# Value products of an attention quad: two key chunks per visit to the 32-column tiling instead of one

## The chip, the cores and the metric

The kernel runs on one core of one Trainium2 chip. The metric is the device time of one execution in microseconds (us). A measured time is the median of several executions; beside it stands one execution that was taken with the hardware profiler, and every row of a trace comes from that one.

## The reference

The input is 8 sequences of 512 tokens with 128 features. There is one attention block with 16 heads of 8 features, and one mixture-of-experts block. Cut to what matters here:

```python
qkv = (x @ w_qkv + b_qkv).reshape(B, 16, S, 24)      # B=8, S=512
q, k, v = jnp.split(qkv, 3, axis=-1)
attn = softmax(einsum('bhqd,bhkd->bhqk', q, k) / sqrt(8))
vals = einsum('bhqk,bhkd->bhqd', attn, v)
x = layernorm(x + vals @ w_out + b_out)
# then: a shared expert for each token, 8 routed experts of which each token
# takes 2, a weighted sum, and a second layernorm
```

## The kernel before

**Quads and stages.** The attention works through 32 quads: 8 batches (b) of 4 quads (i = 0 to 3), and a quad is four heads over 512 query and 512 key positions. All engines run the same loop of stages (`run_stages`, line 308). Stages 8 to 27 are a hardware loop of five batches, the others are written out. Stage q = 4b + i does work for several quads at once, as a software pipeline: the score maxima of quad q+2, the exponentials of quad q, the value products of quad q-1, and small jobs for others. In this document "quad 0" to "quad 3" mean the stages with i = 0 to 3.

**A stage on TensorE** (`attention_tensor`, line 955) has eight steps, `at` = 0 to 7. Two steps belong to one value of j (= `at // 2`), and u = `at % 2`. Each step issues four matrix products of 512 columns in bfloat16:
- A, A' (`score_a`, line 971): scores for the row maximum, into a pair of PSUM banks of `scoreA`. There are two pairs, one for even and one for odd steps. VectorE takes the maximum over a pair with one instruction (line 915) and so frees it. So A of step n waits until the maximum of step n-2 is done.
- B, B' (`score_b`, line 985): scores the other way round, each into one of the two banks of `scoreB`. ScalarE turns each into exponentials in SBUF (line 882, 512 elements per partition) and frees the bank. So B of step n waits for the exponential of B of step n-1, and B' for that of B'.

**Small jobs** follow the four products of a step (`Jobs.at`, line 71). They share one PSUM bank, `shared`, so a job on TensorE waits until the reader of the job before it is done (line 499). In every quad: mT at step 1 (line 520; VectorE reads it after its maximum of step 1, lines 595 and 597), valsT at step 3 (line 524; VectorE reads it after its maximum of step 3), xT at step 4 (line 502), and the three projections qkv at step 6 (lines 508, 509, 513; read by ScalarE). In quad 1 also counts at step 2 (line 493; VectorE reads it with lines 380 and 383) and oT at step 7; in quad 2 proj at step 0; in quad 3 x1T at step 5 and gate at step 7. VectorE also has the routing's arithmetic: `choose` in quad 0 (line 318) and `place` in quads 1 and 2 (line 393), small instructions put behind its maxima at odd steps. Batches 2 and later have routing; batches 1 and later have the layer norm's statistics.

**The value products** are at the end of a step (lines 999 to 1008). At u = 1, so behind steps 1, 3, 5 and 7, four products for key chunk j are issued, one for each head h. Their weights have 32 columns each and go to columns 32h to 32h+31, so that the four stand beside each other in the array, and their results to 32 partitions of the bank `pvp` each. The operands are float32, and the trace has two MATMUL records for each product (8 for a chunk). Every other product of a step uses all columns. The four chunks of a quad add up in PSUM (start at j = 0, stop at j = 3). ScalarE copies the finished bank to `pv_sb` at the start of the next stage (line 874). The first products of a quad wait for `exp_done` (the exponentials of the quad are finished), `v_ready` (the values, from GpSimd) and `pv_copied` (the bank has been copied).

Below, a "visit" is the run of column-tiled value products between two other products.

```python
                    score_a(at, 0)
                    score_b(at, 0)
                    score_a(at, 1)
                    score_b(at, 1)
                    for kind in jobs.at(b, i, at):
                        pe_job(pe, kind, b, i)
```

After the attention (about 512 us into the span) come the shared expert and 72 blocks of routed rows. The change does not touch them.

Of the kernel before, what the change touches and what calls it, by code (L numbers as in the profile page):

```python
# [103 lines left out]
def layer(nc, x, w_qkv, b_qkv, w_out, b_out, wg, ws1, ws3, ws2, we1, we3, we2, out):  # L104
# [26 lines left out]
    with ctx:  # L131
        def sb(name, shape, dt=F32):
            return ctx.enter_context(nc.sbuf_tensor(name, shape, dt))

        def psum(name, shape):
            return ctx.enter_context(nc.psum_tensor(name, shape, F32))
# [42 lines left out]
        v = sb("v", [P, 2, 4, NCH, 32])  # L179
        prob = sb("prob", [P, 2, 4, NCH, 512])  # L180
# [52 lines left out]
        pvp = psum("pvp", [P, 512])  # L233
# [52 lines left out]
        def need(eng, s, value):  # L286

            if isinstance(value, int) and value <= 0:
                return
            eng.wait_ge(s, value)  # L290
            if not isinstance(value, int) and eng.engine in ALONE:


                eng.sem_inc(passed, 1)

        def has(b, i, ahead):

            return not isinstance(b, int) or 0 <= 4 * b + i + ahead < QUADS
# [9 lines left out]
        def run_stages(eng, stage):  # L308

            for s in range(-4, 8):  # L310
                stage(s // 4, s % 4)
            with eng.Fori(2, B - 1) as b:
                for i in range(4):
                    stage(b, i)
            for s in range(QUADS - 4, QUADS + 1):
                stage(s // 4, s % 4)
# [355 lines left out]
        def turn_x(pe, b):  # L672

            pe.wait_ge(x1_loaded[b], 16)

            need(pe, xT_low_done, b)
            for c in range(NCH):
                ins = pe.transpose(xT_bank[:, c * P:(c + 1) * P], xsum[:, b, c, :], ident[:])
            ins.then_inc(xT_ready, 1)
# [275 lines left out]
        def attention_tensor(pe):  # L955

            pe.wait_ge(setup, 2)

            def stage(b, i):
                q = 4 * b + i  # L960
                if has(b, i, 2):

                    pe.wait_ge(stack_loaded[i % 2], 16 * STACK_DMAS * (2 * b + i // 2 + 2))
                def score_a(at, c):

                    if has(b, i, 2):
                        st, j, qc = (i + 2) % 4, at // 2, at % 2 * 2 + c

                        if c == 0:
                            need(pe, max_done, 8 * (q + 2) + at - 1)  # L970
                        ins = pe.matmul(scoreA[:, at % 2, c], qs[0:KR, st, j, qc * P:(qc + 1) * P],  # L971
                                        ks[0:KR, st, j, :], start=True, stop=True)
                        if c == 1:
                            ins.then_inc(a_ready, 1)

                def score_b(at, c):

                    if has(b, i, 0):
                        j, kc = at // 2, at % 2 * 2 + c
                        if at == 0 and c == 0:  # L980

                            pe.wait_ge(m_loaded, 32 * (q + 1))

                        need(pe, exp_done, 16 * q + 2 * at + c - 1)
                        pe.matmul(scoreB[:, c], ks[0:KM, i, j, kc * P:(kc + 1) * P], qs[0:KM, i, j, :],  # L985
                                  start=True, stop=True).then_inc(b_ready, 1)

                for at in range(8):
                    j, u = at // 2, at % 2
# [6 lines that stand above are left out]

                    if isinstance(b, int) and q == QUADS and at == 4:
                        turn_x(pe, 0)
                    if u == 1 and has(b, i, -1):
                        if j == 0:  # L1000
                            pe.wait_ge(exp_done, 16 * q)
                            pe.wait_ge(v_ready, q)
                            need(pe, pv_copied, q - 1)
                        for h in range(4):
                            ins = pe.matmul(pvp[32 * h:32 * h + 32, :], v[:, (i - 1) % 2, h, j, :],  # L1005
                                            prob[:, (i - 1) % 2, h, j, :], start=(j == 0), stop=(j == 3))
                        if j == 3:
                            ins.then_inc(pv_done, 1)

            run_stages(pe, stage)  # L1010


# [535 lines left out]
```

## Time and profile before

| what | value |
|---|---|
| median of 3 executions | 717.0 us (715.78 to 718.37) |
| profiled execution | 719.39 us, of which the span from first to last instruction is 717.2 us |
| mean granted TensorE clock | 0.979 of full speed; full in the steady attention |
| attention's value products | from 58.8 us to about 511.9 us in the span |
| a batch of four quads in the steady loop | 58.2 us |

The profiled execution took 2.4 us more than the median. A time for the changed kernel is to be read against the median, while durations and starts come from the profiled execution. In the timeline a row is: start, duration, engine, line, operation, output<-inputs, count; in square brackets how long the engine was idle before it, and what ended this. Rows for MATMUL run into each other: a product of 512 columns lasts 0.38 us in the records while the next one starts 0.22 us behind it. The distance from start to start is what TensorE's time is counted in. PEld is the load of weights.

### The profile page before, as it was taken

The page shows a single profiled execution, that of the slowest core. Times are in us where ns is not written, and L with a number is a line of the kernel's source. Part 1 is how long each engine was busy: PE and PEld are TensorE (multiplying, and loading weights), DVE is VectorE, ACT ScalarE, POOL GpSimd, SP SyncE. Part 2 cuts the span into 40 slices and gives each one's busy share as a digit, 9 for nine tenths or more (in the row PEclk, how much of TensorE's full clock was granted, in tenths as well). Part 3 has the DMA queues.
Part 4 walks back from the last instruction along what each step waited for, and adds up shares of the span by engine and source line. Part 5 has one row for each costly group of instructions (what it writes and reads, how often), then busy time and mean ns, then how long its engine had stood idle before and what let it go on. Part 6 is the DMA issues. An engine that isn't in the chain of part 4 may idle for free.

```text
span 717.2 us, 16568 instructions
## 1 busy us (share of the span) xinstructions
PE 649.3 (91%) x4593; PEld 312.3 (44%) x4594; DVE 543.9 (76%) x1208; ACT 427.0 (60%) x973; POOL 273.5 (38%) x418
## 2 busy tenths in 40 slices
PE   1899999999999999999999999998999898788870
PEld 1242333333343434334343334232488676666650
DVE  4965777779988997997997998876587566666651
ACT  1055767766777676766777677667342455555541
POOL 3112312322144243434225414505155265665562
PEclk9999999999999999999999999999899999998995
DMA  4357577354333334234323333301320233433321
GB/s 79 69 127 170 112 148 149 79 103 95 83 74 87 59 86 97 57 56 110 85 48 82 85 84 74 75 2 56 108 60 29 63 83 106 142 114 112 111 73 59
DMA packets 161848, 62.58 MB, mean 87 GB/s; under 512 B 110586, under 2 KB 155516, under 8 KB 161808
## 3 DMA queue, kind: packets, MB, share of 16 engines
q1 hardware_dynamic: 154112, 48.55, 30.5%
q0 software_dynamic: 5648, 13.26, 6.2%
q10 hardware_dynamic: 2048, 0.27, 0.3%
q8 instruction: 21, 0.34, 0.2%
q14 instruction: 19, 0.16, 0.1%
HBM read 38.04 MB, written 24.26 MB: 87 GB/s over the span
## 4 chain that ended last, share of the span: by engine, by line
PE 64%; DMA 9%; issue 8%; DVE 7%; POOL 5%; ACT 4%; SPq 1%; POOLq 0%; ACTq 0%; DVEq 0%
PE pvp L1005 17%; PE scoreB L985 16%; PE scoreA L971 15%; DMA y_dram<-prob 3%; DVE mx L915 2%; POOL y_dram L1162 2%; ACT prob L882 2%; DMA parts_dram<-parts 2%; PE shared L524 2%; DMA prob<-slots_dram 2%; PE shared L513 2%; PE scoreB L1490 1%; DMA ks<-parts_dram 1%; PE shared L508 1%; PE shared L532 1%
## 5 line engine op out<-in xcount | busy, mean ns | idle before, releaser
L915 DVE TENSOR_REDUCE mx<-scoreA 128x2 f32<-128x1024 f32 x256 | 305.8, 1220 | 69.8 <-PE scoreA L971 67.3
L882 ACT ACTIVATE prob<-scoreB 128x512 f32<-128x512 f32 x512 | 279.5, 600 | 119.0 <-PE scoreB L985 114.5
L971 PE MATMUL scoreA<-ks,qs 72*128 72x512 bf16 x512 | 206.0, 410 | 13.3 <-DMA ks<-parts_dram 10.9
L985 PE MATMUL scoreB<-qs,ks 74*128 74x512 bf16 x512 | 201.2, 396 | 6.3 <-ACT prob L882 3.0
L1005 PE MATMUL pvp<-prob,v 128*32 128x512 f32 x1024 | 139.8, 619 | 0.8 <-ACT pv_sb L874 0.8
L971 PEld LDWEIGHTS scoreA<-ks,qs 72*128 72x128 bf16 x512 | 51.0, 102 | 155.1 <-DVE mx L915 72.1
L809 POOL CAST parts<-qk 128x256 bf16<-128x256 f32 x32 | 12.7, 395 | 217.7 <-ACT v_raw L562 198.8
L1162 POOL DMA_INDIRECT y_dram<-prob x72 | 71.5, 993 | 60.6 <-ACT prob L1374 31.5
L985 PEld LDWEIGHTS scoreB<-qs,ks 74*128 74x128 bf16 x512 | 49.8, 99 | 102.0 <-ACT prob L882 80.3
L487 POOL DMA_INDIRECT slots_dram<-rows,slot_i x64 | 63.3, 989 | 26.7 <-issue 17.4
L1321 DVE TENSOR_TENSOR prob<-scoreA,prob 128x256 f32<-128x256 f32 x72 | 30.4, 422 | 31.6 <-ACT prob L1368 31.3
L1490 PE MATMUL scoreB<-w,prob 128*128 x288 | 45.4, 282 | 0.1
L1374 ACT ACTIVATE prob<-scoreB,prob 128x128 f32<-128x128 f32 x72 | 26.3, 366 | 31.1 <-PE scoreB L1490 29.8
L1368 ACT ACTIVATE prob<-scoreA 128x256 f32<-128x256 f32 x72 | 27.4, 381 | 22.8 <-PE scoreA L1469 22.8
L1477 PE MATMUL pvp<-ident,prob 128*128 128x128 f32 x144 | 29.1, 284 | 12.2 <-DVE prob L1326 11.6
L1490 PEld LDWEIGHTS scoreB<-w,prob 128*128 128x128 f32 x288 | 38.8, 196 | 0.4 <-issue 0.2
L1467 PE MATMUL scoreA<-w_high,ebT_high 128*128 x72 | 35.3, 491 | 0.9 <-DVE ebT_low L1274 0.9
L1005 PEld LDWEIGHTS pvp<-prob,v 128*32 128x32 f32 x1024 | 20.5, 109 | 30.1 <-issue 28.5
L558 ACT ACTIVATE qk<-shared,bq 128x128 f32<-128x128 f32 x64 | 20.0, 364 | 17.8 <-PE shared L513 12.0
L1326 DVE COPY prob<-pvp 128x256 f32<-128x256 f32 x72 | 29.9, 415 | 0.6 <-PE pvp L1477 0.3
L1477 PEld LDWEIGHTS pvp<-ident,prob 128*128 128x128 f32 x144 | 16.3, 143 | 31.1 <-DVE prob L1321 18.1
L635 POOL TENSOR_SCALAR veps<-mv 128x4 f32<-128x4 f32 x8 | 1.8, 222 | 72.3 <-DVE mv L617 72.3
(172 smaller groups left out, 882.6 us busy)
## 6 DMA issues: line engine op xcount, KB each, us to landing
qs<-parts_dram SPq DMA_DIRECT2D x96, 96.0 KB
parts_dram<-parts SPq DMA_DIRECT2D x32, 192.0 KB, 3.7
slots_dram<-blank POOLq DMA_DIRECT2D x9, 520.0 KB
prob<-slots_dram SPq DMA_DIRECT2D x72, 65.0 KB, 1.9
ks<-parts_dram SPq DMA_DIRECT2D x64, 64.0 KB
prob<-y_dram SPq DMA_DIRECT2D x8, 512.0 KB, 3.2
ks<-parts_dram SPq DMA_DIRECT2D x32, 96.0 KB
xin<-in_L_attn_x SPq DMA_DIRECT2D x32, 64.0 KB, 2.1
```

The source lines that it names most:

```text
L487: pool.indirect_dma_start(slots_dram, bass.IndirectOffsetOnAxis(ap=slot_i[:, j, t:t + 1], axis=0), rows[:, t, j, :], None).then_inc(scatte ...
L882: act.activation(prob[:, i % 2, j, 2 * u + c, :], scoreB[:, c], ACT.Exp, scale=SCALE).then_inc(exp_done, 1)
L915: dve.tensor_reduce(mx[:, i % 2, at // 2, at % 2 * 2:at % 2 * 2 + 2], scoreA[:, at % 2], AX.X, ALU.max).then_inc(max_done, 1)
L971: ins = pe.matmul(scoreA[:, at % 2, c], qs[0:KR, st, j, qc * P:(qc + 1) * P], ks[0:KR, st, j, :], start=True, stop=True)
L985: pe.matmul(scoreB[:, c], ks[0:KM, i, j, kc * P:(kc + 1) * P], qs[0:KM, i, j, :], start=True, stop=True).then_inc(b_ready, 1)
L1005: ins = pe.matmul(pvp[32 * h:32 * h + 32, :], v[:, (i - 1) % 2, h, j, :], prob[:, (i - 1) % 2, h, j, :], start=(j == 0), stop=(j == 3))
L1162: pool.indirect_dma_start(y2_dram, bass.IndirectOffsetOnAxis(ap=eb[:, r, D:D + 1].bitcast(I32), axis=0), yo[:, r, :], None, bounds_check=T ...
L1321: dve.tensor_tensor(gated[:, r % 2, :], scoreA[:, 0, r % 2, F:2 * F], silu[:, r % 2, :], ALU.mult) \
L1326: dve.tensor_copy(gatedT[:, (r - 1) % 2, :], pvp[:, 0:F]).then_inc(gT_copied, 1)
L1467: pe.matmul(h, ebT_high[:, r % 2, 0:P], high, start=True, stop=False)
L1477: ins = pe.transpose(pvp[:, c * P:(c + 1) * P], gated[:, (r - 1) % 2, c * P:(c + 1) * P], ident[:])
L1490: ins = pe.matmul(y, gatedT[:, r % 2, c * P:(c + 1) * P], w2_flat[:, bass.ds(e * NFC * D + c * D, D)], start=(c == 0), stop=(c == NFC - 1))
```

## The change

The visits behind steps 1 and 5 are taken away. The visit behind step 3 issues the products of chunks 0 and 1, that behind step 7 those of chunks 2 and 3. The three waits of a quad's first value product stand ahead of the visit behind step 3. Number, shape and order of the value products stay the same.

```diff
-                    if u == 1 and has(b, i, -1):
-                        if j == 0:
+                    if u == 1 and j % 2 and has(b, i, -1):
+                        if j == 1:
                             pe.wait_ge(exp_done, 16 * q)
                             pe.wait_ge(v_ready, q)
                             need(pe, pv_copied, q - 1)
-                        for h in range(4):
-                            ins = pe.matmul(pvp[32 * h:32 * h + 32, :], v[:, (i - 1) % 2, h, j, :],
-                                            prob[:, (i - 1) % 2, h, j, :], start=(j == 0), stop=(j == 3))
+                        for kc in (j - 1, j):
+                            for h in range(4):
+                                ins = pe.matmul(pvp[32 * h:32 * h + 32, :], v[:, (i - 1) % 2, h, kc, :],
+                                                prob[:, (i - 1) % 2, h, kc, :], start=(kc == 0), stop=(kc == 3))
                         if j == 3:
                             ins.then_inc(pv_done, 1)
```

## Rows read from the trace of the kernel before

**Rows 1.** The page: busy time of each engine; shares of the last chain by line.
```profile
PE 649.3 (91%) x4593; PEld 312.3 (44%) x4594; DVE 543.9 (76%) x1208; ACT 427.0 (60%) x973; POOL 273.5 (38%) x418
...
PE pvp L1005 17%; PE scoreB L985 16%; PE scoreA L971 15%; DMA y_dram<-prob 3%; DVE mx L915 2%; POOL y_dram L1162 2%; ACT prob L882 2%; DMA parts_dram<-parts 2%; PE shared L524 2%; DMA prob<-slots_dram 2%; PE shared L513 2%; PE scoreB L1490 
```

**Rows 2.** Busy time by stretch: quads 2, 3, 0 and 1 of the steady loop.
```profile
245.17:259.55 14.38, 14.35 (x119) 5.78 (x115) 13.48 (x30) 9.90 (x21) 3.20 (x7) 1.00 0.28 60
259.55:274.77 15.22, 15.07 (x123) 6.11 (x119) 12.28 (x23) 10.60 (x24) 7.45 (x11) 1.00 0.39 91
274.77:288.49 13.72, 13.58 (x111) 4.71 (x107) 12.26 (x24) 9.89 (x21) 5.56 (x8) 1.00 0.45 101
288.49:303.38 14.89, 14.75 (x119) 5.58 (x115) 13.64 (x32) 10.40 (x23) 5.95 (x11) 1.00 0.29 58
```

**Rows 3.** The page's costliest groups: maxima, exponentials, value products.
```profile
L915 DVE TENSOR_REDUCE mx<-scoreA 128x2 f32<-128x1024 f32 x256 | 305.8, 1220 | 69.8 <-PE scoreA L971 67.3
L882 ACT ACTIVATE prob<-scoreB 128x512 f32<-128x512 f32 x512 | 279.5, 600 | 119.0 <-PE scoreB L985 114.5
...
L1005 PE MATMUL pvp<-prob,v 128*32 128x512 f32 x1024 | 139.8, 619 | 0.8 <-ACT pv_sb L874 0.8
```

**Rows 4.** Timeline, end of the attention: chunks 2 and 3 of the last quad.
```profile
509.95 1.93 PE L1005 MATMUL pvp<-prob,v 128*32 128x512 f32 x16
...
510.41 0.13 PEld L1005 LDWEIGHTS pvp<-prob,v 128*32 128x32 f32 x4 [0.30 <-issue]
...
511.81 0.50 PE L1437 MATMUL scoreA<-ebT_high,w_high 128*128 128x512 f32 x1
```

**Rows 5.** Timeline of quad 0, first half: steps 0 and 1 and the visit.
```profile
274.77 0.39 PE L971 MATMUL scoreA<-ks,qs 72*128 72x512 bf16 x1
...
275.49 2.16 ACT L882 ACTIVATE prob<-scoreB 128x512 f32<-128x512 f32 x4
275.63 2.38 DVE L915 TENSOR_REDUCE mx<-scoreA 128x2 f32<-128x1024 f32 x2 [1.83 <-PE scoreA L971]
...
276.14 0.39 PE L985 MATMUL scoreB<-qs,ks 74*128 74x512 bf16 x1
...
276.63 0.39 PE L985 MATMUL scoreB<-qs,ks 74*128 74x512 bf16 x1
...
277.06 1.06 PE L1005 MATMUL pvp<-prob,v 128*32 128x512 f32 x8
...
278.06 0.39 PE L971 MATMUL scoreA<-ks,qs 72*128 72x512 bf16 x1
```

**Rows 6.** Timeline of quad 0, second half: its start, step 5, its visit.
```profile
281.60 0.39 PE L971 MATMUL scoreA<-ks,qs 72*128 72x512 bf16 x1
...
282.91 2.35 DVE L915 TENSOR_REDUCE mx<-scoreA 128x2 f32<-128x1024 f32 x2
...
283.38 0.39 PE L985 MATMUL scoreB<-qs,ks 74*128 74x512 bf16 x1
...
283.70 1.07 PE L1005 MATMUL pvp<-prob,v 128*32 128x512 f32 x8
...
284.70 0.39 PE L971 MATMUL scoreA<-ks,qs 72*128 72x512 bf16 x1
```

**Rows 7.** Timeline of quad 1: counts, its read, valsT, start of the second half.
```profile
292.83 0.40 PE L493 MATMUL shared<-both,lower 128*128 128x32 f32 x2
...
293.98 0.19 DVE L383 COPY count<-shared 128x32 f32<-128x32 f32 x1
...
294.23 0.66 PE L524 MATMUL shared<-ident,pv_sb 128*128 128x128 f32 x4
...
295.81 0.39 PE L971 MATMUL scoreA<-ks,qs 72*128 72x512 bf16 x1
```

**Rows 8.** Timeline of the last quad with exponentials: two steps, no A.
```profile
492.88 0.60 PE L985 MATMUL scoreB<-qs,ks 74*128 74x512 bf16 x2
493.31 2.17 ACT L882 ACTIVATE prob<-scoreB 128x512 f32<-128x512 f32 x4 [0.72 <-PE scoreB L985]
```

## The prediction

> **What bounds the kernel now.** I read the page first. TensorE is busy for 91% of the span, VectorE for 76%, ScalarE for 60%, and the chain that ended last names the value products at 17% and the two kinds of scores at 16% and 15% [rows 1]. Next the busy time by stretch, one for each quad of the steady loop: TensorE is busy in nearly all of it (13.58 of 13.72 us in quad 0), but VectorE in 12.26 to 13.64 us of 13.72 to 15.22 [rows 2]. So TensorE sets the pace with VectorE just behind it. Then the groups: a maximum takes 1.22 us, an exponential 0.60 [rows 3]. Last the timeline, where I count from start to start.
>
> **What a visit costs.** The last B' ahead of the visit in quad 0 starts at 283.38, the visit at 283.70, the next A at 284.70 [rows 6]. Between two score products stand 0.22 us, so going in costs 0.32 - 0.22 = 0.10, and a visit 1.00. How two chunks in a row do shows at the end of the attention, where no scores stand between them: 16 records from 509.95, the next product at 511.81, which is 1.86 us against 2 x 1.00 [rows 4]. A chunk adds 0.86 and coming out costs 0.14. A merge saves one way in and one out, 0.10 + 0.14, say 0.23 us. There are 1024 records, 8 for each of 128 visits [rows 3]; 64 merges, of which one is in effect already there, leave 63 x 0.23 = **14.5 us** of TensorE's time to be had at most. Waits of the first visit (exponentials, values, copied bank) come later than now and can only shrink. No DMA, job or instruction of another engine is moved, and SP and POOL keep their order.
>
> A rule speaks against this price. The Trainium skill's "TensorE: Matmul & The Clock Gate" (Part 3, the mechanism) says that a weight load overlaps products in flight only when it goes to other rows of the array, and these loads use all rows. The rows say otherwise: the four loads at 510.41 lie inside the running products, and the 1.86 us has room for none outside. By the rule the sum would be worse by some 16 us (a rival below).
>
> **What the visits cover.** Now to what a visit does for the others. Taking B of one step and B of the next, the loop through one bank is: product to exponential 0.43 (492.88 to 493.31 [rows 8]), exponential 0.60 [rows 3], and 0.06 until the next product starts. That is 1.08 us for a step, and four products in a row need only 4 x 0.22 = 0.88. For VectorE a step costs 1.19 (two maxima in 2.38 [rows 5]). So TensorE outruns both inside a run of steps, and the visit is when they catch up. After a one-chunk visit the first step runs free and the second waits (B at 276.14, 1.37 behind the half's first A, where 1.10 would be free [rows 5]). Take visit 1 away, and steps 2 and 3 run at the others' pace too.
>
> **First half of a quad** (steps 0 to 3, first A = 0). B and B' of step 1 start at 1.37 and 1.86 as now [rows 5]. Those of step 2 follow 1.08 later (2.45, 2.94), those of step 3 at 3.53 and 4.02; mT, 0.11 long, lies in a wait. A of step 2 needs maximum 0, done at 275.63 + 1.19, so 2.05: it is not late. A of step 3 needs maximum 1 at 3.24: starts at 3.30, which moves B' to at most 4.06. The scores end at 4.28, valsT takes 0.53, the visit 1.86: **6.67** against 281.60 - 274.77 = 6.83 now [rows 5, 6], so -0.16. A quad without routing has 6.63 against 6.75: -0.12.
>
> **Second half** (A of step 4 = 0). xT fits in as now. Exponential 5 ends at 2.36 and 2.88, so step 6 has B at 2.42, B' at 2.94; qkv takes 0.93, step 7 0.88, into the visit at 5.06, **6.92** at the end, against 6.89 now: +0.03. The waits of step 6, which visit 2 used to cover, take back all of the 0.23.
>
> **Quad 0 with routing.** VectorE has `choose` between the maxima and starts maximum 4 at 282.91 whatever TensorE does (it is without a gap from maximum 2 on), done at 284.09. A of step 6 could now start at 283.44 but waits to 284.15; now visit 2 fills that time, to 284.70 [rows 6]. From 284.15 on: step 6 0.88, qkv 0.93, step 7 0.88, way in 0.10, visit 1.86 gives 288.81, against 288.49 now: **+0.32**.
>
> **Quad 1 with routing** is the costliest. counts waits until VectorE has read mT (it starts at 292.83), and valsT until VectorE has read counts (293.98 + 0.19, it starts at 294.23) [rows 7]. Both waits are 0.2 us or less today, with visit 0 ahead of them. That chain does not get shorter by moving visit 0 behind it. It comes 0.18 earlier (VectorE's step 7 and 0 come up earlier), so valsT starts at 294.05, 0.58 to the visit, 1.86: A of step 4 at 296.49 against 295.81, +0.68 [rows 7]. In the second half oT waits for ScalarE's read of qkv and ends 7.61 later against 7.57. So it leaves at +0.72, of which quad 1 adds **+0.40**.
>
> **Quads 2 and 3.** In quad 2 proj (0.89 us) stands in step 0 and lets the others catch up; the same walk gives -0.24 and +0.03: **-0.21**. In quad 3 VectorE's first maximum comes at 1.18, holding A of step 2 to 2.42 and A of step 3 to 3.59: +0.05; x1T's read holds qkv by 0.17 in the second half, and the half gives -0.06: **-0.01**.
>
> **The sum.** A batch: 0.32 + 0.40 - 0.21 - 0.01 = +0.50. Five batches (2 to 6): +2.5. The first two quads of batch 7: +0.7. Its other two have no A and go at ScalarE's pace: eight exponentials in 2.17 a four, idle 0.72 before each four [rows 8], so 5.76 a half where now two visits cover them, 5.9 with one, less 0.2 at proj: +0.3. Quads 2 to 7 of the count, mostly without routing: -0.6. The first, at a clock half as fast with 1.86 for a one-chunk visit, so that nobody outruns anybody: -0.3. The last, without scores: -0.2. Together +2.4 us: **14.5 us of switching saved, about 17 us of waits exposed**. The profiled execution was 719.39, 2.4 above the median of 717.0; a difference carries over, so 717.0 + 2.4 = **719.4 us**.
>
> The unknown is how the waits add up: each of some four a quad was rounded with a latency of 0.06, and could be 0.02 to 0.10 (the exponential's measured answer is the nearest row); that and the phases it moves make 0.15 a quad, 4.5 us in all: 715 to 724 for this case.
>
> **Rivals.** *Gain (0.15).* The engines catch up in the two-chunk visit enough that waits stay as they are; speaking for it, VectorE has 0.9 to 2.9 us of a quad free and ScalarE 3.8 to 4.6 [rows 2]. Then 717.0 - 14.5 = 702.5; with half of it given back, 710. It is decided by step 6: does B start 1.1 or 1.3 behind the B of step 5. Against it: the loop of 1.08 is a latency, which no free time shortens. The Trainium skill's "TensorEngine Tiling (Array Packing)" (PSUM Bottleneck) speaks against it too: tiling makes TensorE faster but not the engines that empty PSUM, which may then be the limit. By it alone nothing of the 14.5 would arrive, and the time would stay at 717.0.
>
> *Loss by VectorE (0.17).* VectorE starves in the long visit (it has at most two maxima, 2.4 us, stored, often one) and falls behind in all quads as in quad 1. Then each of 30 quads adds 0.4: +12, 729 us. It decides where maximum 3 or 7 ends over 0.7 us before the next A pair is ready. For it: VectorE needs 13.5 of 14.38 us in quad 2. Against: in quad 2 the gap after maximum 7 exists already.
>
> *Weight loads exposed (0.03).* Loads of 0.13 [rows 4] ahead of the two later waves of each merged visit, 62 x 2 x 0.13 = 16 us on top: 735. By the rule of the Trainium skill's "TensorE: Matmul & The Clock Gate" named above it would be so.
>
> *The change saves no switch (0.03):* if what costs 0.14 is paid per chunk, a merged visit is 2.00 long: +9 on top, 728. Against it stands the 1.86 of [rows 4].
>
> **Numbers.** My case has 0.62. The range takes it and part of the gain case and of the loss case: 711 to 726. A measurement can tell 0.3%, 2.15 us. Faster: 0.15 from the gain and 0.04 of mine, 0.19. Slower: 0.17 + 0.06 and 0.25 of mine, 0.48. Same 0.33.
>
> **What would show it.** Merged visits of 16 records, 1.86 to the next product; 64 of them. Steps 2, 3 and 6 with B waiting for the exponential 0.1 to 0.3; in quad 0, A of step 6 waiting for the maximum by 0.7; in quad 1, counts waiting by 0.7 for the read of mT. Quads of 13.5 (no routing), 14.0, 15.3, 14.2 and 15.2 us (quads 0 to 3). A batch under 58.0 us would make me wrong, as would B of step 2 running free, or a merged visit near 2.0 us.

## The result, and the profile after

The changed kernel takes 729.08 us (median of 4 executions, 724.70 to 732.53) against 716.39 for the kernel before on the same chip (4 executions, 713.64 to 718.37): a ratio of 1.0157, 95% interval 1.0103 to 1.0211. (The ratios in this text are estimated from the single executions and are not the quotients of the medians; here the quotient is 1.0177, or 12.7 us.) It is slower, by more than the forecast of 719.4 and outside the range that ended at 726. Its profiled execution took 724.70 us, with a span of 722.5 and a mean granted TensorE clock of 0.975; the other three had 0.960, 0.964 and 0.969.

First the page of the changed kernel: busy time, shares of the last chain by line, the costliest groups.

```profile
PE 647.1 (90%) x4593; PEld 319.3 (44%) x4594; DVE 542.5 (75%) x1208; ACT 426.2 (59%) x973; POOL 274.9 (38%) x418
...
PE pvp L1006 14%; PE scoreB L985 13%; PE scoreA L971 13%; DVE mx L915 5%; DMA y_dram<-prob 3%; ACT prob L882 2%; PE shared L524 2%; PE scoreB L1491 2%; PE shared L513 2%; POOL y_dram L1163 1%; DMA prob<-slots_dram 1%; PE shared L508 1%; PE 
...
L915 DVE TENSOR_REDUCE mx<-scoreA 128x2 f32<-128x1024 f32 x256 | 303.9, 1217 | 76.7 <-PE scoreA L971 74.6
L882 ACT ACTIVATE prob<-scoreB 128x512 f32<-128x512 f32 x512 | 279.8, 602 | 98.2 <-PE scoreB L985 97.7
...
L1006 PE MATMUL pvp<-prob,v 128*32 128x512 f32 x1024 | 129.0, 623 | 0.0
```

Against [rows 1, 3]: the value products are as many (1024) and cover 10.8 us less, 129.0 for 139.8, since fewer switches lie among them. The chain now goes through the maxima for 5% of the span instead of 2%: TensorE waits for VectorE where it did not.

Next the busy time by stretch, for quads 2, 3, 0 and 1 of the same batch as in [rows 2]; the columns are the stretch, its length, the busy time of TensorE, weight loads, VectorE, ScalarE and GpSimd, the granted clock, the DMA share and GB/s.

```profile
248.13:262.30 14.17, 14.17 (x118) 5.90 (x115) 12.84 (x28) 9.90 (x21) 3.35 (x6) 1.00 0.30 61
262.30:277.45 15.15, 14.87 (x123) 6.26 (x119) 12.02 (x21) 10.48 (x23) 7.41 (x11) 1.00 0.41 92
277.45:291.49 14.04, 13.35 (x111) 4.94 (x107) 12.77 (x26) 9.90 (x21) 5.60 (x8) 1.00 0.43 99
291.49:307.13 15.64, 14.68 (x119) 5.79 (x115) 14.18 (x33) 10.39 (x22) 5.79 (x12) 1.00 0.27 55
```

| quad | before [rows 2] | forecast | after |
|---|---|---|---|
| 2 | 14.38 | 14.17 | 14.17 |
| 3 | 15.22 | 15.21 | 15.15 |
| 0 | 13.72 | 14.04 | 14.04 |
| 1 | 14.89 | 15.29 | 15.64 |
| batch | 58.21 | 58.71 | 59.00 |

Three quads came out as walked; quad 1 added 0.75 instead of 0.40. But 0.8 us more in each of some six batches is 5 us, not 12.7. The timeline shows the waits of quads 0 and 1, and something that the sum did not hold.

```profile
286.84 0.39 PE L971 MATMUL scoreA<-ks,qs 72*128 72x512 bf16 x1 [0.59 <-DVE mx L915]
...
289.63 1.92 PE L1006 MATMUL pvp<-prob,v 128*32 128x512 f32 x16
291.49 0.39 PE L971 MATMUL scoreA<-ks,qs 72*128 72x512 bf16 x1
...
294.00 0.39 PE L971 MATMUL scoreA<-ks,qs 72*128 72x512 bf16 x1 [0.17 <-DVE mx L915]
...
294.66 0.38 PE L985 MATMUL scoreB<-qs,ks 74*128 74x512 bf16 x1
295.72 0.40 PE L493 MATMUL shared<-both,lower 128*128 128x32 f32 x2 [0.68 <-DVE m L597]
...
299.53 0.39 PE L971 MATMUL scoreA<-ks,qs 72*128 72x512 bf16 x1
...
174.56 0.63 PE L493 MATMUL shared<-both,lower 128*128 128x32 f32 x2 [0.68 <-DVE m L597]
...
178.11 3.51 PE L1006 MATMUL pvp<-prob,v 128*32 128x512 f32 x16
...
354.72 0.40 PE L493 MATMUL shared<-both,lower 128*128 128x32 f32 x2 [0.68 <-DVE m L597]
...
357.62 2.51 PE L1006 MATMUL pvp<-prob,v 128*32 128x512 f32 x16
```

The merged visit is 291.49 - 289.63 = 1.86 us, as in [rows 4]. `A` of step 6 in quad 0 is idle for 0.59 before it starts, `counts` in quad 1 for 0.68. Counted from start to start these waits are longer: `counts` starts 1.06 behind `B'` at 294.66 where 0.22 would be free, so it loses 0.84, and `A` of step 6 loses 0.75 in the same way (286.84 against `B'` at 285.87). Then look at the same quad in two other batches, at 174 and 355: after the same wait, `counts` at 174.56 takes 0.63 us for 0.40, and the merged visit 3.51 and 2.51 instead of 1.92. The busy time by stretch around the second of them has the reason in its granted clock:

```profile
352.00:354.00 2.00, 1.84 (x8) 0.56 (x6) 2.00 (x3) 1.72 (x4) 1.72 (x6) 1.00 0.41 43
354.00:356.00 2.00, 1.32 (x8) 0.83 (x8) 1.93 (x6) 0.72 (x2) 1.23 (x1) 0.86 0.52 55
356.00:358.00 2.00, 2.00 (x10) 1.09 (x12) 1.51 (x3) 1.19 (x2) 0.00 (x0) 0.50 0.34 105
358.00:360.00 2.00, 2.00 (x16) 0.32 (x8) 1.11 (x7) 0.00 (x0) 0.00 (x0) 0.79 0.60 158
```

TensorE, busy 1.32 us of the 2 with the wait, falls from full clock (2.4 GHz) to the half (1.2 GHz) and works there for about 3 us; at 174 it is about 7 us. I call this a clock fall. The half quad with it took 9.57 us at 350 and 11.22 at 170, against 8.04 without: 1.5 and 3.2 us. From here on the text counts only falls between 70 and 490 us: in the last two quads or behind them every profile has stretches at half clock, the kernel before too (0.50 from 504 to 508 us). The attention's products end 6.8 us later than before (518.63 against 511.81); the two falls are 4.7 of that and the waits 2.1, where 2.4 was forecast. The part behind the attention is 1.5 us shorter (203.9 against 205.4), so the span has +5.3. The profiled execution before had 719.39, so the forecast stood for 721.8 there, and 724.7 came: +4.7 of falls, -0.3 of waits, -1.5 behind the attention. The other three executions have no profile, but a lower granted clock. A clock lower by 0.010 means 2% of the span, 14.5 us, at half clock, and half of that lost, about 7 us (an estimate); their mean lies 5.5 us above the profiled one. Where they lost the clock is not shown.

### The profile page after: what moved, and what is told of

Read it like the earlier page. It is cut to its first block, busy times and chain, and to the rows that moved or that the text cites. A ratio compares the mean times of both kernels' runs of the same rounds, so it can differ in the third digit from the quotient of the medians.

```text
span 722.5 us, 16563 instructions
## 1 busy us (share of the span) xinstructions
PE 647.1 (90%) x4593; PEld 319.3 (44%) x4594; DVE 542.5 (75%) x1208; ACT 426.2 (59%) x973; POOL 274.9 (38%) x418
## 4 chain that ended last, share of the span: by engine, by line
PE 59%; DVE 12%; issue 10%; DMA 7%; POOL 5%; ACT 4%; SPq 1%; POOLq 0%; DVEq 0%; ACTq 0%
PE pvp L1006 14%; PE scoreB L985 13%; PE scoreA L971 13%; DVE mx L915 5%; DMA y_dram<-prob 3%; ACT prob L882 2%; PE shared L524 2%; PE scoreB L1491 2%; PE shared L513 2%; POOL y_dram L1163 1%; DMA prob<-slots_dram 1%; PE shared L508 1%; PE pvp L1478 1%; PE scoreA L1468 1%; DMA parts_dram<-parts 1%
## 5 line engine op out<-in xcount | busy, mean ns | idle before, releaser
L1006 PE MATMUL pvp<-prob,v 128*32 128x512 f32 x1024 | 129.0, 623 | 0.0
L809 POOL CAST parts<-qk 128x256 bf16<-128x256 f32 x32 | 12.7, 396 | 217.7 <-ACT v_raw L562 198.5
L487 POOL DMA_INDIRECT slots_dram<-rows,slot_i x64 | 63.5, 992 | 27.5 <-issue 18.2
L1006 PEld LDWEIGHTS pvp<-prob,v 128*32 128x32 f32 x1024 | 27.4, 112 | 56.0 <-issue 50.8
L874 ACT ACTIVATE pv_sb<-pvp 128x512 f32<-128x512 f32 x31 | 18.5, 597 | 39.6 <-PE pvp L1006 39.6
```

Source lines behind the costliest of these rows:

```text
L487: pool.indirect_dma_start(slots_dram, bass.IndirectOffsetOnAxis(ap=slot_i[:, j, t:t + 1], axis=0), rows[:, t, j, :], None).then_inc(scatte ...
```

## The experiments

Theory 1, the one held after reading the result: the waits are those of the forecast, and the rest is clock falls behind the wait of `counts` in quad 1. Rival 2: the ratio is switching and waits alone, and the falls are chance that the kernel before has too. Rival 3: VectorE falls behind everywhere. Most kernels put the two `if` lines of the visit behind a table from step to key chunks; what differs is its content:

```diff
-                    if u == 1 and j % 2 and has(b, i, -1):
-                        if j == 1:
+                    chunks = visits(i).get(at, ())
+                    if chunks and has(b, i, -1):
+                        if chunks[0] == 0:
...
-                        for kc in (j - 1, j):
+                        for kc in chunks:
...
-                        if j == 3:
+                        if chunks[-1] == 3:
```

The kernel before is {1: 0, 3: 1, 5: 2, 7: 3} in this form ("four"), the changed one {3: 0 1, 7: 2 3} ("two"). The experiments ran on two other chips, the first four of the table on one, the others on the second. There the kernel before itself takes 741.35, 743.29 and 741.17 us (medians beside the three groups), so only ratios compare with the result; the times in us that the expectations of the first four runs give are meant for the first chip.

| run | visits | median us | ratio to before, 95% |
|---|---|---|---|
| again | two | 745.61 | 1.0040 (1.0007 to 1.0074) |
| first_pair | {3: 0 1, 5: 2, 7: 3} | 754.00 | 1.0157 (1.0105 to 1.0210) |
| second_pair | {1: 0, 3: 1, 7: 2 3} | 740.48 | 0.9968 (0.9928 to 1.0007) |
| not_quad1 | four in quad 1, else two | 737.07 | 0.9866 (0.9795 to 0.9937) |
| twin | four (one run) | 741.00 | - |
| cover | see below | 759.73 | 1.0263 (1.0185 to 1.0341) |
| filler | two, with products in the wait | 738.60 | 0.9933 (0.9897 to 0.9970) |
| pool_light | two, lighter split (one run) | 737.56 | - |
| best_b | four in quad 1, three in quad 0, else two | 731.82 | 0.9871 (0.9781 to 0.9960) |
| only_quad1 | two in quad 1, else four | 758.35 | 1.0226 (1.0110 to 1.0341) |
| early | {1: 0 1, 5: 2 3} | 768.36 | 1.0313 (1.0204 to 1.0423) |
| again_b | two | 745.57 | 1.0057 (1.0015 to 1.0098) |

### The change once more: again, again_b

> The changed kernel once more, in more rounds, to see how its executions spread. Theory 1 (waits in fixed places, of which the wait of counts in quad 1 also lets TensorE's clock fall in some batches): about 728 us, single executions from 724 to 733, and the mean granted clock between 0.96 and 0.975, lower in the longer executions, against 0.979 before. Theory 2 (the long visit starves ScalarE and VectorE everywhere alike, the clock has no part): the executions lie within 2 us of each other, with one clock.

> The changed kernel beside the others on this chip. Ratio 1.004 if ScalarE is late in quad 3 on this chip too (B of step 5 then waits over 1 us in the kernel before and 0.45 here), 1.016 if it is not. The clock falls after the wait of counts in one to six batches of a profile.

The change is slower here too, but by 0.4 and 0.6%, less than the 1.6% of the first chip. The falls are there: in the profile of again three batches took 62.54, 60.90 and 60.91 us, the others 58.70 to 59.37, and again_b has three falls too. Over all executions the mean granted clock is 0.961 in again and 0.960 in again_b, against 0.969 to 0.973 for the kernel before beside the three groups. Five of these six falls follow `counts` in quad 1. The sixth, the 60.91 of again, does not: it follows the wait of `A` of step 6 in quad 0 of the last batch.

```profile
466.52 0.39 PE L971 MATMUL scoreA<-ks,qs 72*128 72x512 bf16 x1 [0.66 <-DVE mx L915]
...
470.29 3.64 PE L1006 MATMUL pvp<-prob,v 128*32 128x512 f32 x16
```

Why the ratio is smaller, the next run shows.

### The kernel before on this chip: twin

> The kernel before itself, profiled on the same chip as the runs beside it. Theory 1: its quads are as on the other chip (batch 58.2 us, no fall of TensorE's clock inside the steady attention, every B of step 4 followed by its exponential after 0.42 us). If the chip itself delays ScalarE in quad 3 (0.9 us instead of 0.42 after B of step 4, as all profiles of the last call show), the delay stands in this trace too. Theory 2, that the merges cause this delay: it is absent here.

Its batches take 59.8 us where the first chip took 58.2. By stretch, quad 3 of the kernel before on this chip:

```profile
258.08:274.55 16.47, 15.15 (x122) 6.11 (x119) 12.47 (x23) 10.62 (x24) 7.44 (x11) 1.00 0.36 84
```

Quad 3 takes 16.47 instead of the 15.22 of [rows 2]. Its timeline:

```profile
323.49 1.15 ACTq L891 DMA_DIRECT2D qs<-m  x2
...
325.40 0.38 PE L985 MATMUL scoreB<-qs,ks 74*128 74x512 bf16 x1
...
326.61 1.08 ACT L882 ACTIVATE prob<-scoreB 128x512 f32<-128x512 f32 x2 [2.61 <-PE scoreB L985]
...
327.27 0.39 PE L985 MATMUL scoreB<-qs,ks 74*128 74x512 bf16 x1 [1.16 <-ACT prob L882]
```

The exponential starts 1.21 us behind its product's start (0.43 in [rows 8]), and the next `B` waits 1.16 for it. It is the first one behind two DMA issues on ScalarE's queue. In the merged kernel the long visit covers most of this: its quad 3 takes 15.41 here (again_b, below). So on this chip the change is paid back 1.06 us a batch, where the first chip gave 0.07; over the whole batch it is 1.3 us (59.84 to some 59.4 here, 58.21 to 59.00 there). The late exponential stands only in the five batches of the hardware loop (in batch 1 quad 3 takes 15.09 on both chips), so that makes 6 us, 0.8 to 0.9%: 1.0157 less this is 1.007 to 1.008, against the 1.004 and 1.006 measured. Why ScalarE is late on these chips stays open. It is also not the whole difference of the chips: the profiled span is 738.8 against 717.2, and 12.7 us of that stand behind the attention; their cause is open.

### One half merged: first_pair, second_pair

> Only chunks 0 and 1 are merged (behind step 3); chunks 2 and 3 stand behind steps 5 and 7 as before. Theory 1: first halves of -0.20, +0.72, -0.24 and -0.19 us (quads 0 to 3) give nearly nothing a batch, but the wait of counts stays and with it the falls of the clock: 718 to 724 us, with a clock under 0.975 in some executions. Theory 2 (all merges cost alike): half of the loss of 11.3, 722 us, with no quad better than before.

> Only chunks 2 and 3 are merged (behind step 7). Theory 1: second halves of +0.52, +0.03, +0.03 and +0.12 us (quads 0 to 3), +0.70 a batch, some +4 us in all, 720 to 722 us; visit 0 stands ahead of counts again, so the clock is 0.978 as before and executions lie close together. Theory 2: half of the loss, 722 us.

Both are misses: the times expected stand for ratios of 1.002 to 1.011 and 1.005 to 1.008. Merging chunks 0 and 1 alone costs 1.6%, more than the whole change on the same chip (again, 1.0040). The wait of `counts` comes with the missing visit 0, and a clock fall followed it in each of the five batches of the loop (61.4 to 63.5 us each), where again had two there; and with a one-chunk visit in quad 3 the late exponential stays uncovered (16.36 us against 15.51 in again). Merging 2 and 3 alone costs and gains nothing that can be told (0.9968), and has no fall. That is a net: against twin its quad 0 is 0.4 longer and its quad 3 0.6 to 0.7 shorter, the latter a gain that only a chip with the late exponential has. So what hurts most is in the first half. Rival 3 would have had both halves lose.

### Quad 1 alone, and all but quad 1: only_quad1, not_quad1

```diff
+                return two if i == 1 else four      (only_quad1, shortened)
+                return four if i == 1 else two      (not_quad1, shortened)
```

> The merged visits in quads 0, 2 and 3 only; quad 1 has its four visits. Theory 1: -0.20 and +0.52 in quad 0, -0.21 in quad 2, -0.07 in quad 3, so nothing a batch to within 0.1, and no falls of the clock: 716 to 719 us, clock 0.978. Theory 2: three quarters of the loss, 725 us.

> The other way round: merged visits in quad 1 alone. Theory 1: quad 1's first half 7.9 to 8.1 us instead of 7.3, with the clock falling in some or most batches after the wait of counts; six quads of 32 are changed and the time is 5 to 12 us over the kernel before, ratio 1.007 to 1.016, mean clock under 0.972. Theory 2 (all merges cost alike): a quarter or less of the loss, ratio 1.001 to 1.004.

The two bracket it. Without the merge in quad 1 the kernel is faster than before, by 1.3% in the comparison and by 0.6% in the medians, more than the nothing that was expected, since quad 3 is covered here (15.5 us). With the merge in quad 1 alone it is 2.3% slower, again more than expected. The timeline of only_quad1, quad 1:

```profile
359.48 0.39 PE L974 MATMUL scoreA<-ks,qs 72*128 72x512 bf16 x1 [0.42 <-DVE mx L915]
...
360.14 0.38 PE L988 MATMUL scoreB<-qs,ks 74*128 74x512 bf16 x1
361.20 0.59 PE L493 MATMUL shared<-both,lower 128*128 128x32 f32 x2 [0.67 <-DVE m L597]
```

and by stretch:

```profile
358.70:360.70 2.00, 1.40 (x6) 0.46 (x5) 2.00 (x3) 1.46 (x4) 1.98 (x5) 1.00 0.19 20
360.70:362.70 2.00, 1.50 (x6) 1.12 (x7) 1.77 (x5) 0.51 (x2) 1.52 (x2) 0.64 0.74 79
362.70:364.70 2.00, 2.00 (x7) 1.04 (x5) 1.23 (x2) 1.20 (x2) 0.00 (x0) 0.50 0.17 52
```

The wait of `counts` is as in the changed kernel (0.67), but the `A` before it waits 0.42 instead of 0.17, with four visits in quad 0 (that TensorE comes out of them further ahead of VectorE is my reading, not shown). With the two waits together the fall comes in five of six batches, and here so early that `counts` itself is already slow (0.59 for 0.40). The sixth, batch 2, is the best control: `counts` waits the same 0.68, but `A` before it does not wait, and no fall comes.

```profile
172.92 0.39 PE L974 MATMUL scoreA<-ks,qs 72*128 72x512 bf16 x1
...
174.64 0.40 PE L493 MATMUL shared<-both,lower 128*128 128x32 f32 x2 [0.68 <-DVE m L597]
```

Over the five batches of the loop in all profiles, where `A` waited 0.28 to 0.42 and `counts` 0.67 or 0.68 behind it, a fall came in 8 of 8 batches (only_quad1, first_pair); where `A` waited 0.15 to 0.17, in 8 of 16 (the change, again, again_b, first_pair). With this rival 2 falls as well: the six profiles without this pair of waits, or with products in the second (before, twin, second_pair, not_quad1, best_b; filler), have no fall in 36 batches.

### The falls without the waits' idle time: filler

Four throwaway products fill the time in which `counts` waits. The waits for data stay as long as they are; TensorE only isn't idle in them.

```diff
+                    if i == 1 and at == 2 and routing(b) and has(b, i, 0):
+                        need(pe, pv_copied, q - 1)
+                        for _ in range(4):
+                            pe.matmul(pvp[:], ks[0:KM, i, 1, 0:P], qs[0:KM, i, 1, :], start=True, stop=True)
                     for kind in jobs.at(b, i, at):
                         pe_job(pe, kind, b, i)
```

> The changed kernel, with four products of 512 columns whose results are thrown away (they go to the free bank of the value products, before its first real one) put ahead of counts in quad 1, where TensorE else waits 0.84 us. They take 0.88 us and add at most 0.1 us a batch of their own. Theory 1 (the clock falls because TensorE idles there): no fall in the steady attention, first half of quad 1 at 8.05 to 8.15 us in every batch, and 3 to 7 us less than the changed kernel, a ratio of about 1.00 on a chip like the last. Theory 2 (the clock falls for another reason, or falls cost nothing): as the changed kernel or slower by 0.7 us.

By stretch, quads 3 and 1 of again_b (the change):

```profile
262.26:277.67 15.41, 14.96 (x123) 6.28 (x119) 12.13 (x21) 10.48 (x23) 7.42 (x11) 1.00 0.40 90
...
291.70:308.90 17.20, 16.23 (x119) 6.35 (x115) 14.29 (x33) 10.51 (x22) 5.79 (x12) 0.90 0.26 50
```

and of filler:

```profile
288.24:303.88 15.64, 15.37 (x122) 6.18 (x119) 14.18 (x33) 10.39 (x22) 5.78 (x12) 1.00 0.27 55
```

Quad 1 takes 15.64 us, what it takes in the changed kernel's batches without a fall, at clock 1.00; with a fall it is 17.20 at 0.90. No batch of filler has a fall (58.7 to 59.4 us), its mean granted clock over ten executions is 0.973, and the kernel that does more work is 7 us faster than the change on the same chip: 0.9933 against 1.0057 (and 1.0040 on the other). The falls cost 1.1 to 1.2%, 7 to 9 us of the median. That is the missing term; it was not measured on the first chip.

### What made quad 1 longer than forecast: pool_light

GpSimd's split of the queries and keys of quad 0 handles an eighth of the elements and leaves the rest of the split out.

```diff
-                    pool.tensor_copy(parts[:, :, :, 0, :], qk32[:]).then_inc(split_step, 1)
+                    n_k = 1 if i == 0 and not isinstance(b, int) else 2
+                    n_h = 1 if i == 0 and not isinstance(b, int) else 4
+                    pool.tensor_copy(parts[:, 0:n_k, 0:n_h, 0, :], qk32[:, 0:n_k, 0:n_h]).then_inc(split_step, 1)
...
```

> The changed kernel, but in quad 0 of the loop GpSimd's four instructions that split queries and keys (lines 809 to 815) work on one eighth of their elements; the other elements stay what an earlier quad left, so the scores of those quads are not the reference's. Theory: VectorE's last five instructions of choose are stretched by GpSimd's running beside them (1.85 us from the first to the next maximum, 1.31 in the kernel before), and this makes the missing 0.36 us of quad 1. Then the five take 1.2 to 1.4 us here, the first maximum of quad 1 comes 0.4 earlier and its first half takes 7.6 to 7.7 us instead of 8.04. Rival: the instructions wait for something else (their data, the semaphores); then nothing moves.

The cause looked for stands in the changed kernel's timeline, VectorE and GpSimd at the start of quad 1, the last five instructions of `choose`:

```profile
290.70 0.67 POOL L811 TENSOR_TENSOR qkr<-qk,parts 128x256 f32<-128x256 f32 x1 [0.19 <-POOL parts L809]
290.87 0.55 DVE L363 TENSOR_TENSOR hot<-iota_e,pick 128x32 f32<-128x32 f32 x1
...
291.56 0.39 DVE L368 TENSOR_TENSOR tot<-top 128x4 f32<-128x4 f32 x1
...
292.11 0.67 POOL L815 TENSOR_TENSOR parts<-qkr,parts 128x256 bf16<-128x256 f32 x1 [0.18 <-POOL parts L813]
292.30 0.51 DVE L373 SCALAR_TENSOR_TENSOR rows<-top,tot 128x8 f32<-128x8 f32 x1
292.72 2.34 DVE L915 TENSOR_REDUCE mx<-scoreA 128x2 f32<-128x1024 f32 x2
```

and the same with the light split:

```profile
288.04 0.18 DVE L363 TENSOR_TENSOR hot<-iota_e,pick 128x32 f32<-128x32 f32 x1
...
288.87 0.17 DVE L373 SCALAR_TENSOR_TENSOR rows<-top,tot 128x8 f32<-128x8 f32 x1
289.53 2.36 DVE L917 TENSOR_REDUCE mx<-scoreA 128x2 f32<-128x1024 f32 x2 [0.48 <-PE scoreA L976]
```

Three small instructions take 0.39 to 0.55 us while an instruction of GpSimd's split runs beside them (0.67, or 0.40 for the one at 291.53), and 0.15 to 0.18 otherwise. The five take 1.85 us (290.87 to 292.72), against 1.31 before, where only one of them was stretched. Without the overlap the first half of quad 1 takes 7.67 us, against 8.04 in the change and the 7.68 of the forecast. The light split takes away more than the added 0.54, but the rest does not count: the first maximum now waits 0.48 for TensorE. So the walk through quad 1 was right but for this overlap. The idle time before `counts` stays (0.55), and with it one fall in six batches (60.53 us).

### Versions meant to keep both gains: cover, early, best_b

What each step issues, in short:

```diff
+                {2: (0, 1), 7: (2, 3)} in quad 1, that visit ahead of counts;
+                {3: (0, 1), 5: (2, 3)} in quad 0; else two          (cover)
+                {1: (0, 1), 5: (2, 3)} in all quads                 (early)
+                four in quad 1; {3: (0, 1), 5: (2,), 7: (3,)} in quad 0; else two   (best_b)
```

> Merged visits everywhere, but in quad 1 chunks 0 and 1 stand behind the scores of step 2 and ahead of counts, and in quad 0 chunks 2 and 3 stand behind step 5. So each of the two large waits (counts for the read of mT, 0.84 us; A of step 6 for the maximum, 0.75 us) lies under a visit. Theory 1: both waits are gone, no fall of the clock, quad 1's first half 7.2 us instead of 8.04, quad 0's second half 6.7 to 7.0 instead of 7.41; a batch of 57.5 to 57.9 us; ratio to the kernel before 0.99 to 1.00. Theory 2 (long visits starve the others wherever they stand): no better than the changed kernel, a ratio above 1.004.

> All four quads merged, the visits behind steps 1 and 5 instead of 3 and 7, so the same number of switches saved as in the changed kernel and again four steps between visits. Theory 1 (what counts is whether VectorE's chain mT, counts, valsT and its work in quad 0 lie under a visit): the visit stands ahead of counts and of step 6, so neither of the two large waits appears and quad 1's first half is 7.3 to 7.5; but steps 6, 7, 0 and 1 now run without a visit, and mT may wait for VectorE by some 0.5 us in quad 1; the ratio is 0.99 to 1.005, below the changed kernel on the same chip. Theory 2 (number and length of visits alone count): the same as the changed kernel within 0.3%.

> Merges only where the half-quads measured so far gain: chunks 0 and 1 in quads 0, 2 and 3, chunks 2 and 3 in quads 2 and 3; quad 1 keeps four visits. Theory 1: against the run without quad 1 this takes quad 0's wait of A of step 6 away (0.75 us, of which 0.5 net): a batch of 57.6 to 57.8 us where the kernel before has 58.2, or 58.0 to 58.3 where it has 59.8; no fall of the clock in the steady attention; ratio 0.98 to 0.995, the fastest of all. Theory 2 (long visits starve the others): not under 1.00.

Cover is a miss. With a visit ahead of it, `counts` does not wait, but between the visit at step 5 of quad 0 and that at step 2 of quad 1 lie five steps without one:

```profile
294.44 0.39 PE L988 MATMUL scoreB<-qs,ks 74*128 74x512 bf16 x1 [0.30 <-ACT prob L882]
...
297.49 0.39 PE L974 MATMUL scoreA<-ks,qs 72*128 72x512 bf16 x1 [0.59 <-DVE mx L915]
...
298.46 3.59 PE L1006 MATMUL pvp<-prob,v 128*32 128x512 f32 x16
```

The waits stand elsewhere (a third of 0.37 lies between the two shown), 1.3 us in three pieces, and a fall comes behind them in all six batches (visit 3.59). The ratio alone would fit theory 2; it is the timeline that names waits and clock. The second half of quad 1 is longer too (8.65 for 7.60). Early is a miss and the slowest of all (1.0313), outside what either theory gave it: `counts` waits nowhere in the loop, but `B` in quad 0 waits 0.71 and the clock falls there; a batch takes 65.0 us in its profile, 5 more than in twin, some 3 of them in quad 0 with its fall and the rest by waits in the other quads. Best_b leaves the merge out where a half had lost (quad 1, and the second half of quad 0), and has no fall:

```profile
240.65:254.81 14.16, 14.16 (x118) 5.90 (x114) 13.46 (x32) 9.90 (x21) 3.87 (x8) 1.00 0.30 61
254.81:270.33 15.52, 14.95 (x122) 6.27 (x119) 12.14 (x21) 10.48 (x23) 7.42 (x11) 1.00 0.39 90
270.33:283.85 13.52, 13.41 (x111) 4.77 (x107) 12.24 (x24) 9.88 (x21) 4.94 (x7) 1.00 0.45 103
283.85:298.74 14.89, 14.75 (x119) 5.58 (x115) 13.65 (x32) 10.42 (x23) 5.96 (x11) 1.00 0.30 58
```

58.09 us a batch against 59.84 in twin, 0.9871 of the kernel before: it beats both kernels, as not_quad1 does (58.6 us a batch). Of the 1.75 us, 0.95 are quad 3, where the merge covers ScalarE's late start. On the first chip, quads 2 and 3 of the change and quads 0 and 1 of best_b would make 14.17 + 15.15 + 13.52 + 14.89 = 57.73 against 58.21, some 0.5% in all (an estimate; best_b was not run there).

## Why the prediction was wrong

**The price of a visit: right.** A merged visit is 1.86 us, 0.23 less than two. The Trainium skill's "TensorE: Matmul & The Clock Gate" (Part 3, the mechanism), by which the loads would stand outside the products, gave 735 us; the 1.86 contradicts it, however near the median came to that time.

**Quads 2, 3 and 0: right**, to 0.06 us each, and so is the first half without routing, to 0.07 (6.56 measured, 6.63 forecast). The waits came at the forecast places: from start to start `A` of step 6 in quad 0 loses 0.75 (0.7 forecast), `counts` in quad 1 loses 0.84 (0.7).

**"Quad 1 with routing ... adds +0.40": mis-sized**, it measured +0.75. The prediction let VectorE's chain come up 0.18 earlier with the durations that it had. It came up earlier, and so lay beside GpSimd's split, which stretched it by 0.54 (pool_light). Five batches make 1.8 us of that.

**The sum: right in what it held.** Without the two falls the attention is 2.1 us longer, 2.4 forecast. That this is so near is partly luck: the five batches of the loop gave 3.0 us instead of 2.5, though a DMA wait of 0.74 in the kernel before (at 172.1) did not come back, and the others -0.9 instead of -0.1: the six quads from 2 on gave -1.1 for -0.6, and the first two of batch 7 +0.3 for +0.7.

**The step that failed: the sum has no term for TensorE's clock.** The price of a half clock was put at nothing. "The first, at a clock half as fast" was read as the start's matter only; all later durations were taken at full clock, since the kernel before shows 1.00 in the steady attention [rows 2]. The prediction itself made `counts` wait 0.7 us behind a quad 0 that waits 0.7, but priced these waits as their length. They also cost the clock, at 1.5 to 3.2 us a time in the profiled execution: 4.7 us there, 7 to 9 us of the median on the other chips. That is more than the 2.1 us that switches and waits come to together.

**The rivals.** The gain did not come: `B` of step 2 starts 2.45 behind the quad's first `A` and `B` of step 3 at 3.53, both as walked. "Loss by VectorE", with 729 us, has the measured time by another way: quads 2 and 3 lost nothing (14.17 and 15.15), so it is not 0.4 in each of 30 quads. It is quads 0 and 1 (+0.32 and +0.75), and the clock behind them. That a merge saves no switch is out by the 1.86.

## What to carry to other kernels

Work that stands between two runs of a tight producer and consumer loop pays its switch, but hides the loop's latencies; before batching it, walk each stretch that is left without it, and leave the merge out where a chain of another engine ends in that stretch. Where an edit opens waits close together on TensorE (here 0.68 us behind 0.17, or behind 0.42), price them at the clock that follows, not at their length, and read the granted clock by stretch, not as a mean over the span (0.979 and 0.975 hid it). Here a small instruction of VectorE with two inputs lasted until the GpSimd instruction that it met had ended; when an edit moves one past the other, the durations of before don't carry over.

## What the runs showed of the hardware

- The granted clock fell to half behind waits of less than 1 us: 0.68 with one of 0.15 to 0.17 ahead in 8 of 16 batches, 0.67 with one of 0.28 to 0.42 ahead in 8 of 8. It fell behind 0.55 alone in one of five batches (pool_light), behind 0.66 in quad 0 once (again), and not behind 0.68 alone (one batch of only_quad1). With products in the wait of `counts` it did not fall. The Trainium skill's "TensorE: Matmul & The Clock Gate" (A second HAM failure mode) tells of a kernel in which short idles between groups of products let the clock swing; the runs agree with it. As a rival it would have turned the two waits into a price. What decides between batches with equal waits is open.
- An instruction of VectorE with two inputs that met one of GpSimd ended right behind it: `hot` at 291.42 behind GpSimd's at 291.37, `rows` at 292.81 behind 292.78. Such instructions on 128x4 to 128x32 took 0.39 to 0.55 us instead of 0.15 to 0.18; RECIPROCAL, with one input, took its 0.18 at 289.38 in the kernel before while GpSimd's CAST ran from 289.40 to 289.80. The Trainium skill's "SBUF — State Buffer" (SBUF: two separate sides) says that the two engines share one pair of ports, held for a whole instruction, and that VectorE needs it for two SBUF inputs while GpSimd reads SBUF; the rows agree.
- The same kernel took 716 to 717 us on one chip and 741 to 743 on two others. In the profiles 1.25 us in each of five batches stand in one place, a late exponential on ScalarE, and 12.7 us behind the attention; neither has a cause yet.
